# Second attention of a two-layer model on one NeuronCore: block-diagonal global keys, stationary global exponentials, layer norm on ScalarE

## The reference

```python
Q = (x @ Wq.T + bq).reshape(Bb, Ll, H, Dh)      # 16 heads of 8, also K and V
s_loc = einsum('blhd,blwhd->bhlw', Q, Kw)*scale # window of 65 keys around each token
local = einsum('bhlw,blwhd->blhd', softmax(where(valid, s_loc, NEG_INF)), Vw)
Kg, Vg = K[:, global_indices], V[:, global_indices]   # 25 keys
s_g = einsum('blhd,bghd->bhlg', Q, Kg) * scale
glob = einsum('bhlg,bghd->blhd', softmax(s_g), Vg)
out = (0.7 * local + 0.3 * glob) @ Wo.T + bo
x = layernorm(x + out)
```

## Time and profile before

| | |
|---|---|
| runs | 1098.07, 1108.61, 1110.83 us; median 1108.61 |
| profiled execution | 1103.31 us |
| its span | 1101.6 us |
| mean granted TensorE clock | 0.924 of 2.4 GHz |
| second attention, from the first to the last gathering of global keys | 453.3 to 815.6 us |

### The profile page before, as it was taken

The page is one execution under the profiler, slowest core; times in us unless marked ns, Lnnn a source line. Parts: engine busy times, 40 slices in busy tenths (PEclk is TensorE's granted clock), DMA queues, the critical chain, the costliest instruction groups (busy, mean ns, idle before and its releaser), DMA issues.

```text
span 1101.6 us, 27734 instructions
## 1 busy us (share of the span) xinstructions
PE 953.2 (87%) x7536; PEld 699.0 (63%) x7536; DVE 781.5 (71%) x3615; ACT 577.6 (52%) x1250; POOL 678.9 (62%) x1491
## 2 busy tenths in 40 slices
PE   3999999999959995799999999999999319999940
PEld 1777777777735552677777777777776218777830
DVE  3788888888825776457786877777775327888846
ACT  2566676666621332255555555555545007777734
POOL 3566666666631322266769888887879523777765
PEclk9899999999978998599999999999989559999975
DMA  6121111211042441111112121212211166777717
GB/s 184 27 52 32 45 45 31 48 27 45 23 132 91 161 164 80 32 47 34 47 29 59 39 59 48 68 44 60 53 32 38 44 173 234 238 234 250 254 58 212
DMA packets 71375, 98.34 MB, mean 89 GB/s; under 512 B 13688, under 2 KB 43256, under 8 KB 71104
## 3 DMA queue, kind: packets, MB, share of 16 engines
q1 hardware_dynamic: 61040, 83.31, 25.9%
q0 software_dynamic: 4992, 10.30, 2.8%
q10 hardware_dynamic: 5232, 3.42, 1.2%
HBM read 49.48 MB, written 24.77 MB: 67 GB/s over the span
## 4 chain that ended last, share of the span: by engine, by line
PE 73%; DVE 10%; issue 5%; DMA 3%; POOL 3%; ACT 2%; SPq 2%; DVEq 0%; ACTq 0%; POOLq 0%
PE bank L342 6%; PE bank L172 5%; PE bank L253 5%; PE bank L351 4%; PE bank L372 4%; PE bank L1491 4%; PE bank L1492 4%; PE bank L1257 4%; PE bank L1493 4%; PE bank L406 4%; PE bank L168 3%; PE bank L413 3%; PE bank L346 3%; PE bank L381 3%; PE bank L398 2%
## 5 line engine op out<-in xcount | busy, mean ns | idle before, releaser
L528 ACT ACTIVATE p<-bank 128x480 f32<-128x480 f32 (+1 forms) x448 | 240.5, 540 | 247.8 <-PE bank L372 88.0
L663 DVE CUSTOM_DVE_ANT_0 bank<-bank,band 128x160 f32<-128x160 f32 x512 | 156.9, 347 | 82.0 <-PE bank L342 79.5
L663 DVE CUSTOM_DVE_ANT_0 bank<-bank,causal 128x128 f32<-128x128 f32 (+1 forms) x512 | 169.4, 386 | 56.1 <-PE bank L346 40.3
L893 POOL TENSOR_SCALAR_AFFINE_SELECT p<-p 128x380 f32<-128x380 f32 (+1 forms) x256 | 146.5, 602 | 57.2 <-ACT p L528 56.2
L1669 POOL DMA_INDIRECT y_rows<-p,rows x92 | 105.9, 1151 | 67.5 <-DVE p L1622 46.2
L663 DVE DVE_READ_ACCUMULATOR2_ANT nm<- 128x1 f32 x1024 | 143.6, 140 | 0.1
L874 POOL TENSOR_SCALAR_AFFINE_SELECT p<-p 128x256 f32<-128x256 f32 (+1 forms) x192 | 91.0, 486 | 68.3 <-ACT p L528 64.6
L342 PE MATMUL bank<-ks,qs 128*128 128x186 f32 x512 | 118.6, 316 | 3.5 <-issue 2.3
L342 PEld LDWEIGHTS bank<-ks,qs 128*128 128x128 f32 x512 | 81.5, 198 | 38.2 <-issue 23.3
L372 PE MATMUL bank<-qs,ks 128*128 128x160 f32 x512 | 102.2, 303 | 0.0
L1562 ACT ACTIVATE p<-bank,wb 128x512 f32<-128x512 f32 x92 | 63.6, 691 | 39.5 <-PE bank L1493 37.6
(11 more groups left out here) (207 smaller groups left out, 2330.0 us busy)
## 6 DMA issues: line engine op xcount, KB each, us to landing
qs<-parts SPq DMA_DIRECT2D x46, 512.0 KB, 5.2
qs<-qf SPq DMA_DIRECT2D x128, 128.0 KB, 2.4
rows<-xr SPq DMA_DIRECT2D x23, 260.0 KB, 3.7
parts<-ks SPq DMA_DIRECT2D x8, 512.0 KB, 2.8
xs<-x_b SPq DMA_DIRECT2D x16, 256.0 KB, 4.0
p<-in_w SPq DMA_DIRECT2D x12, 256.0 KB, 3.4
xin<-in_x SPq DMA_DIRECT2D x16, 128.0 KB, 2.2
parts<-qf SPq DMA_DIRECT2D x4, 512.0 KB, 2.7
```

The lines of the kernel that those rows point to most:

```text
L528: act.activation(pb[:, :, :].rearrange("p u c -> p (u c)")[:, lo:lo + cols], bank[:, 0:cols], ACT.Exp, scale=SCALE).then_inc(L.exp_done, 1)
L663: return dve.tensor_tensor_reduce(at, at, mask, -1.0, -BIG, ALU.add, ALU.min, nm[:, item:item + 1])
L893: pool.affine_select(out=at, in_=at, compare_op=ALU.is_ge, fill=0.0, base=base, pattern=[[0, 4], [sign, hi - lo]], channel_multiplier=-sig ...
```

## The change

Global scores: `lay_out_kg` (new, DVE at (1,2)) lays the 25 keys of four heads out block-diagonally, 4x25 in 128 columns, by a multiplication with `diag`. `pass2(j,3)` exists only for j = 2 and 3; it takes two heads' groups each, with 128x128 weights and 256 columns of unspread queries from a ring of three `qf` buffers, into which the maxima rows are now sent too (a second transfer behind each first). ACT then takes exp of 128x512 twice instead of 128x256 four times. Global values: `global_values` (new, PE at (0,0) of the next iteration) keeps those exponentials as weights and streams `vgb`, 64 columns, so that the result stands by tokens: no copy to `ogs`, no `round_og`. At the end of an iteration come `round_kg`, `keep_array_busy` (new: two matmuls of the identity) and, on DVE, `keep_kg`. The layer norm of this stage is scaled by ACT (`Identity` with scale and bias) at the iteration's end, with two more small POOL operations; it was DVE's L705 at (3,2). The counts `rp` go from (0,0) to (1,2) of the odd iteration, `positions` from (0,0) to (1,3), `places` to (2,0), the weights to (2,1), and the sends move with them.

```diff
-ROUNDS = (("pj0", "og", "mx0", "ont", "mx1", "y", "q1", "xt", "mx3"),
-          ("rp", "ot", "pj1", "rt", "q0", "vg", "rl", "mx2", "k0", "k1", "kg"))
+ROUNDS = (("pj0", "mx0", "ont", "mx1", "y", "q1", "xt", "mx3"),
+          ("ot", "pj1", "rp", "rt", "q0", "vg", "rl", "mx2", "k0", "k1", "kg"))
...
+        def global_values():
+
+            pe.wait_ge(L.exp_done, L.unit2(i - 1, 3, 3) + 1)
+            pe.wait_ge(L.vg_kept, fin + 1)
+            wait(pe, L.on_done, fin)
+            for tau in range(2):
+                out = T.og[:, tau * S:(tau + 1) * S].rearrange("p (r t z) -> p r t z", r=2, t=4)
+                for t in range(4):
+                    m = pe.matmul(out[:, :, t, :], T.pg[t // 2][:, t % 2 * S + tau * P:t % 2 * S + (tau + 1) * P],
+                                  T.vgb[p][:, t, :].rearrange("p (r z) -> p r z", r=2),
+                                  start=tau == 0 and t == 0, stop=True, skip_group_check=True)
+            m.then_inc(L.pg_done, 1)
...
+        def keep_array_busy():
+
+            wait(pe, L.red_done, L.units * (4 * i + 3) + 3)
+            for _ in range(2):
+                pe.matmul(T.s1[0][:, 0:P], T.ident[:], T.ident[:], start=True, stop=True)
...
                 if L.local:
-                    pe.wait_ge(L.kg_kept, i + 1)
+                    pe.wait_ge(L.kg_kept, 2 * i + 1)
...
             if L.local and u == 3:
-                for t in range(4):
-                    m = pe.matmul(bank[32 * t:32 * t + 32, 0:S], T.kg[par][:, t, :], q[:, t, :].bitcast(F32),
-                                  start=True, stop=True)
+                pe.wait_ge(L.kd_done, i)
+                for c in range(2):
+                    t = 2 * (j - 2) + c
+                    m = pe.matmul(bank[:, c * S:(c + 1) * S], T.kg[n][:, t, :], T.qf[(i - 1) % 3][:, t, :],
+                                  start=c == 0, stop=True, skip_group_check=True)
...
-                m = pe.matmul(T.og[:, r * S:(r + 1) * S], T.vgb[n][:, j, :], pb[:, 3, 0:S],
-                              start=j == 0, stop=False, skip_group_check=True)
...
+        def lay_out_kg():
+
+
+            wait(dve, L.p2_done, L.unit2(i - 1, 3, 3) + 1 if i > 1 else 0)
+            own = [P, 4, 4, NG]
+            keys = T.ks[p][:, :, 0:NG].bitcast(F32).rearrange("p t (o g) -> p t o g", o=1).to_broadcast(own)
+            mask = T.diag[:, ::DH].rearrange("p (a j o) -> p a j o", a=1, o=1).to_broadcast(own)
+            dve.tensor_tensor(T.kg[p].rearrange("p t (j g) -> p t j g", j=4)[:, :, :, 0:NG], keys, mask,
+                              ALU.mult).then_inc(L.kd_done, 1)
...
+        def layernorm():
+            act.wait_ge(L.rstd, L.deviation_steps * (fin + 1))
+            for tau in range(2):
+                act.activation(W.x_next[:, 2 * fin + tau:2 * fin + tau + 1, :], T.r[:, tau:tau + 1, :], ACT.Identity,
+                               scale=T.rs2[:, tau:tau + 1], bias=T.shift[:, tau:tau + 1]).then_inc(L.x_out, 1)
...
-                if j == 3 and u == 2 and th.finish:
+                if j == 3 and u == 2 and th.finish and not L.local:
                     layernorm()
+        if L.local and th.prep:
+            keep_kg()
```

More of the change, by code:

```diff
@@ L91, in __init__, with unit2 @@
             self.steps = 22
+    def unit2(self, i, j, u):
+        if not self.local:
+            return 3 * (4 * i + j - 3) + u
+        if i == 0:
+            return u
+        return 3 + 14 * (i - 1) + (0, 3, 6, 10)[j] + (u if j < 3 or i < B else u - 3)
 class There:
@@ L109, in max_step, with pass2_unit @@
         return self.late if j == 0 else self.scores
+    def pass2_unit(self, local, j, u):
+        if local and u == 3:
+            return self.late and j > 1
+        return self.pass2[j] and u < 3
 def iterations(eng, local, body):
@@ L174, in in_iteration @@
     def in_iteration(name, i, p, th):
-        if name in ("og", "vg", "kg", "rt", "rl", "rp") and not L.local:
+        if name in ("vg", "kg", "rt", "rl", "rp") and not L.local:
             return False
@@ L209, in bank_read @@
             "k1": (L.k_kept, 2 * k + 4), "xt": (L.xt_kept, k + 3),
[L210 removed]
+            "vg": (L.vg_kept if L.local else None, k + 1), "kg": (L.kg_kept if L.local else None, 2 * k + 4)}[last]
         wait(pe, signal, value)
@@ L434, in body @@
                     round_ot()
-                if j == 0 and u == 2 and th.finish and L.local:
-                    round_og()
+                if j == 0 and u == 0 and th.finish and L.local:
+                    global_values()
                 if j == 1 and u == (1 if L.local else 0) and th.finish:
                     round_ont()
+                if j == 1 and u == 2 and in_iteration("rp", i, p, th):
+                    round_rp()
                 if j == 1 and u == 2 and in_iteration("rt", i, p, th):
@@ L450, in body @@
                     round_xt(i + 2, p)
-                if L.local and (j, u) == (3, 3) and th.prep:
-                    round_kg()
                 if u == L.units - 1 and th.max_step(j) and not (L.local and j == 0):
                     round_mx(j)
-                if th.pass2[j]:
+                if th.pass2_unit(L.local, j, u):
                     pass2(j, u)
-                if th.late and u > 0:
+                if th.late and u in (1, 2):
                     pv(j, u - 1)
@@ L462, in body @@
                 round_mx(j)
+        if L.local and th.prep:
+            round_kg()
+            keep_array_busy()
     iterations(pe, L.local, body)
@@ L521, in exp @@
             pb = T.p[(j + 1) % 2]
-            bank = T.s2[u % 2 if L.local else (j + u) % 2]
-            cols = (S if u == 3 else len(local_items(u)) * WIN) if L.local else 512
-            act.wait_ge(L.p2_done, L.units * step + u + 1)
+            unit = L.unit2(i, j, u)
+            bank = T.s2[unit % 2 if L.local else (j + u) % 2]
+            act.wait_ge(L.p2_done, unit + 1)
+            if L.local and u == 3:
+                wait(act, L.pg_done, i - 1)
+                act.activation(T.pg[j - 2], bank[:, :], ACT.Exp, scale=SCALE).then_inc(L.exp_done, 1)
+                return
+            cols = len(local_items(u)) * WIN if L.local else 512
             if u == 0:
                 wait(act, L.pv_done, step - 1)
-            lo = 3 * WIN * u if L.local and u < 3 else 512 * u
+            lo = 3 * WIN * u if L.local else 512 * u
             act.activation(pb[:, :, :].rearrange("p u c -> p (u c)")[:, lo:lo + cols], bank[:, 0:cols], ACT.Exp,
@@ L553, in body @@
                     keep_rt()
-                if j == 0 and u == 1 and L.local and th.pair and p == 1:
+                if j == 0 and u == 2 and L.local and th.pair and p == 1:
                     second_exponential()
@@ L565, in body @@
                 keep_stack(0, j - 1)
+        if L.local and th.finish:
+            layernorm()
     iterations(act, L.local, body)
@@ L1812, in build @@
         Z.mi, Z.hb, Z.yb = [bank[0], bank[1]], [bank[2], bank[3], bank[6], bank[7]], [bank[4], bank[5]]
-        Z.xb = [sb(f"rows{r}", [P, 4, XW])[:, :, :] for r in range(XRING)]
+        Z.xb = [later[:, r * 4 * XW:(r + 1) * 4 * XW].bitcast(F32).rearrange("p (a c) -> p a c", a=4)
+                for r in range(XRING)]
         Z.hh, Z.hl = flat(T.tsr, GT), flat(T.ks[0], GT)[0:2] + flat(T.ks[1], GT)[0:2]
-        Z.xh, Z.xl = flat(T.qf, GT), [sb(f"xl{i}", [P, GT], F32R).ap() for i in range(2)]
+        Z.xh, Z.xl = flat(qf, GT), [sb(f"xl{i}", [P, GT], F32R).ap() for i in range(2)]
         Z.relu, Z.yt = flat(T.p[0], GT)[0:2], flat(T.p[0], GT)[2:4]
```

175 lines of the change are left out of this document (88 added, 87 removed).

## The result

The changed kernel takes 1157.12 us in the median of 4 runs (1144.29 to 1166.46), the kernel before 1107.14 (4 runs beside it, 1098.07 to 1110.83). The ratio is 1.038, 95% interval 1.026 to 1.050: slower, where 1106 with 1086 to 1125 was forecast. The profiled execution took 1163.38 us against 1103.31; over the four the spans are 1142.5 to 1164.7 us and the mean clocks 0.88 to 0.85.

A forecast was written before the change was run, and what follows sets the result against it. TensorE's instruction order was taken to set the pace. Iteration terms, layer norm -4.8 and the end -1.0 summed to -9.7 us; clock falls +7.5 left -2.2. Against the median: 1106 us, range 1086 to 1125.

The forecast's parts named there:

- The clock: Second attention: new TensorE idle stretches make the granted clock fall, taken as five falls at 1.5 us, +7.5 us.
- Rival (a): Second attention: the clock falls in most iterations, twelve more falls at 2.3 us, 1133 us, slower; chance 0.15.
- short waits at L172: TensorE in the kernel before: short waits of 0.2 us at L172 never caused a clock fall.
- no fall at all: Rival (b), second attention: no new clock fall, 1098 us, or 1092 with more layer-norm stalls in the before-like median; chance 0.23.
- The wait for `on_done`: Before the second projection: TensorE idles about 1.6 us; removing work there yields only 0.37 us.
- An iteration without pairs: Second attention, TensorE's removed and added work and waits in a plain or even iteration: -0.35 us.
- Iteration 1: Second attention's iteration with nothing to finish: -2.9 us.
- Counts and places: Odd iterations: q0 waits for `positions` behind DVE's maxima of (1,3), +1.25 us; the iteration +0.75 us.
- The layer norm: Scaling moved from DVE to ACT removes a stall at 812.57 us and slow clock behind it: -4.8 us.
- The warning about `lay_out_kg`: DVE, two SBUF inputs: a POOL mask could hold it; priced 1.1 us of DVE, at most 0.3 us an iteration.
- The end: Iteration 17: bias addition no longer stands behind sends waiting for the pair's routing, residual comes earlier: -1.0 us.

The follow-up runs named there:

- That kernel with a wait: The kernel before with DVE's `normalise` after the maxima of (0,3) instead of (0,2), so TensorE waits longer each iteration; 1138.05 us (1.031).
- the last experiment: Changed kernel with the three waits moved away, `lay_out_kg` at (2,0), two useless matmuls after (0,3) and three after (2,3); 1090.39 us (0.987 to the kernel before).
- The run with the waits removed and the work added: Changed kernel with the three waits moved away, plus useless matmuls, eight after (0,3) and five after (1,3); 1113.55 us (1.008 to the kernel before).
- the one with the work alone: Changed kernel with nothing moved, only useless matmuls added, ten after (0,3) and five after (1,3); 1180.96 us (1.070 to the kernel before).
- theory 1 of the third group: Theory for the runs on the changed kernel with waits removed, work put back, or both: the clock falls where TensorE waits; measured 1.006, 1.070, 1.008.
- the run with the waits removed: Changed kernel with `normalise` after (0,1), counts at (1,1), `positions` at (1,2), weights at (2,0) ahead of `vgb`; 1111.53 us (1.006 to the kernel before).
- the run without the collision: Changed kernel with the three waits moved away and `lay_out_kg` moved from (1,2) to (2,0); 1108.69 us (0.996 to the kernel before).

## Why the prediction was wrong

**The step that failed is "The clock": "I take five at 1.5: +7.5 us".** The mechanism was named there, and the waits that start it; the size was wrong, mainly by the length of a fall. (Nine came in the attention, not five; at 1.5 us each those would be 13.5 us.) The 1.5 us stood for a clock that is down for 3 us, and even the upper price, 2.8, only for the 7 us of the one fall that it was taken from. The changed kernel has 158 us at 1.2 GHz in its attention where before had 22. Against what the other terms give for the attention the loss there is 52.4 + 3.9 = 56 us, or 61 with the layer norm's -4.8, which did not come; for 136 more us at the low clock that is 0.41 to 0.45 us for each. "At most half the time at the lower level" was right, then. That the falls would last 15 us each on average (136 / 9) was not seen. Rival (a), falls in most iterations, had the right mechanism and a chance of 0.15, but was priced from the same fall, at 2.3 us each: 1133 where 1157 came.

**What should have been asked** is what brings the clock back. The fall that the price was taken from happened in a kernel with 3 us more dense plain-fp32 matmuls in an iteration. That kernel with a wait has 0.95 over its attention, the changed one, with waits of the same total, 0.81. I took the recovery over from a kernel that still had what the change removes. The sentence that short waits at L172 never caused a fall overlooked one in the same trace: at 472.3 us the clock fell for some 3 us, behind two waits of 0.20 (before L172 and L296).

The Trainium skill (TensorE: Matmul & The Clock Gate, Why this matters for your kernels) advises against idle gaps between bursts of matmuls, of a length that none of the idle stretches in front of these falls reaches. Here the trace differs: the clock fell behind single waits of 1.4 and 2.0 us and behind a pair of 0.38 and 0.70. A reader who went by that rule alone would have forecast no fall at all, 1098.

**The wait for `on_done`: right.** Forecast 1.6 us of idling in front of the second projection in every finishing iteration; 1.4 us on TensorE's own row (1.6 on the weight load's) in ten of thirteen, and 1.20, 0.15 and 0.15 in the others.

**An iteration without pairs: right, as a sum.** -0.35 us forecast; iterations 2 and 3 take 46.2 instead of 46.9 us, -0.35 each. Iteration 1: -2.9 forecast, 20.4 instead of 23.05 measured.

**Counts and places: right as far as it can be read.** q0 waits 1.06 to 1.16 us for `count`, five times (1.2 forecast). What an odd iteration costs at the full clock the changed kernel never shows.

**The layer norm: the stall went, the gain did not come.** -4.8 us forecast, 0 (-4 to +4) measured by itself. The term assumed that what is behind the stalled operation is late by nothing; another operation with two inputs in the same place took its turn. The sum treated collisions as property of an instruction. They belong to the schedule: L815, L772 (L739 in the kernel with the layer norm alone), L667, and the old scaling L705 each ran at their short time in one kernel and at 1.0 to 2.5 us in another, with the same operands. The warning about `lay_out_kg` (bounded at 1.1 us there) was right in kind: 0.56 to 0.75 us where the change put it, 2.46 us once the timing had moved.

**The end: lost in the clock.** -1.0 forecast; what follows the attention takes 293.1 us at a clock of 0.78; before it was 285.5 at 0.82. In the last experiment, which has this part of the change and a clock of 0.83, it is 283.0. The sign is as forecast, at nearly the same clock; but that run has other edits too, so the size of the term is not shown.

**What of the change's purpose remains.** In the last run the attention takes 350.9 us (16 starts of `pass1(0,0)`, 451.1 to 802.0) against 362.4 before, with five useless matmuls in every iteration. So the change, with its waits moved out of the way, is worth 11.5 us there; the waits that its placing opened cost some five times as much with the falls behind them. How much the kernel before would gain from `normalise` one unit earlier was not run; its own wait there is 0.20 us, thirteen times.

**What stays open.** Why a fall lasts 3 us at one time and 40 at another. In the slow stretches TensorE is busy nearly throughout (38.8 of 40 us), so its busy time does not tell them apart. The run with the waits removed and the work added holds the clock, the one with the work alone does not, so neither alone is the answer; a kernel with long slow stretches and only its dense work varied was not tried (the run with the work put back comes near it, but there L815 had moved under the masks too). Nor is it known why the same wait has a fall behind it in one iteration and none in the next. That "the slow clock keeps itself by making the neighbours late" (theory 1 of the third group) is argued, not shown.

## What to carry to other kernels

Price a new wait on TensorE by what follows it, not by its length: 21 us of waits led to a loss of 52 us here, and removing them without adding work brought four fifths of the loss back. When a change takes work off an engine that sets the pace, look up which waits that work was covering and move their producers in the same edit. And after every move, read the longest duration (not the median) of each short two-input VectorE operation: one of them may now be under GpSimd's masks.

## What the runs showed of the hardware that I had not expected

- A VectorE addition or product with both inputs in SBUF can be held for a whole row of GpSimd instructions, not for one: 128x4 elements took 1.88 us beside four masks that run 2.20 us together, and ended 0.02 us behind the last. The Trainium skill (SBUF — State Buffer, Who interferes with whom) has whoever issues first hold the ports for its instruction; by that, one mask's time (2.20 / 4 = 0.55 us) was all I had expected.
- Not every meeting costs that much. In the run with the waits removed L667 took 0.57 to 0.78 us beside masks, and 2.46 us only where it began 0.17 us behind the first of four in a row. In the run with the early `normalise` L815 took 0.57 us, the length of the first mask, where it began 0.09 us behind the first of three, and 1.88 us where it began 0.34 us behind the first of four.
- The granted clock stayed at 1.2 GHz for 40 us while TensorE was idle for 1.2 us of them.
- Ten executions of one and the same kernel (the run without the collision) differed by 4% (1091 to 1134 us); with five matmuls in idle places six executions differed by 0.9% (1085 to 1095).
